# Moving the experts' first-layer products from the last group of an iteration to its first, in a two-layer attention and mixture-of-experts kernel

## What is computed

```python
xn = _layernorm(x)
s = attention(xn)                # 16 heads of 8 features, causal, softmax over 512 keys
gates = _top_k_softmax(cosine_scores(xn) + xn @ w_route.T, 2)        # 8 experts, top 2
h = jax.nn.gelu(jnp.einsum('bsd,edh->bseh', xn, w1) + b1, approximate=False)   # 8 experts x 64
expert_out = jnp.einsum('bseh,ehd->bsed', h, w2) + b2
g = _silu(jnp.einsum('bse,bsed->bsd', gates, expert_out))
x = x + s * g
xn = _layernorm(x)
s = xn + delta_rule_scan(layernorm_affine(xn))   # a 128x64 state, W -= lr (W k - v) k^T per token
g = _silu(xn @ sign(weight).T)
x = x + s * g
```

## Time and profile before

| | us |
|---|---|
| median of three runs | 613.15 |
| the three runs | 611.65, 613.15, 616.95 |
| time of the profiled execution | 617.68 |
| its span from first to last instruction | 616.0 |
| PE busy | 580.8 |
| DVE busy | 391.8 |
| ACT busy | 351.9 |

### The profile page before, as it was taken

One profiled execution on the slowest core, in us unless ns is written; L12 is line 12 of the kernel. 1 busy time (PEld: TensorE's weight loads), 2 busy tenths in 40 slices (PEclk: granted clock), 3 DMA queues, 4 the chain that ended last, 5 costly groups with the idle time before them and its releaser, 6 DMA issues.

```text
span 616.0 us, 17485 instructions
## 1 busy us (share of the span) xinstructions
PE 580.8 (94%) x7289; PEld 389.4 (63%) x7289; DVE 391.8 (64%) x975; ACT 351.9 (57%) x679; POOL 171.7 (28%) x335
## 2 busy tenths in 40 slices
PE   7799989899998999899999999899998999799897
PEld 3345564567575766677666766678576777565565
DVE  4488765767667676867666685767666675412453
ACT  4412556755675476756675466656675476676231
POOL 7157022412224221432223230432224200311121
PEclk9999999999998999999998999799998999999899
DMA  4766293847252115410362014410361000000001
GB/s 113 162 153 132 44 84 90 157 63 63 74 116 48 43 29 114 97 43 10 87 118 60 10 45 98 95 44 5 83 128 41 10 12 1 26 18 2 3 3 35
DMA packets 58163, 39.42 MB, mean 64 GB/s; under 512 B 17957, under 2 KB 57988, under 8 KB 58084
## 3 DMA queue, kind: packets, MB, share of 16 engines
q1 hardware_dynamic: 58051, 38.29, 30.9%
q10 hardware_dynamic: 32, 0.01, 0.0%
HBM read 24.46 MB, written 9.96 MB: 56 GB/s over the span
## 4 chain that ended last, share of the span: by engine, by line
PE 79%; DVE 11%; ACT 4%; issue 2%; DMA 1%; POOL 1%; SPq 0%; DVEq 0%; POOLq 0%
PE ps_v L950 13%; PE ps_s L930 11%; PE ps_e L911 6%; PE ps_a L865 5%; PE ps_a L851 4%; PE ps_c L1015 4%; DVE cand L1457 4%; PE ps_e L903 3%; PE ps_e L907 3%; PE ps_e L738 3%; PE ps_a L820 3%; PE ps_s L933 2%; PE ps_c L1099 1%; PE ps_c L997 1%; PE ps_c L984 1%
## 5 line engine op out<-in xcount | busy, mean ns | idle before, releaser
L1457 DVE TENSOR_REDUCE cand<-ps_s 128x4 f32<-128x512 f32 (+1 forms) x320 | 213.4, 685 | 74.4 <-PE ps_s L933 45.4
L1251 ACT ACTIVATE prob<-ps_e 128x512 f32<-128x512 f32 x320 | 188.4, 598 | 97.2 <-PE ps_e L911 55.7
L930 PE MATMUL ps_s<-kst,qst 72*128 72x128 bf16 (+2 forms) x1024 | 126.4, 236 | 15.8 <-DVE cand L1457 12.0
L930 PEld LDWEIGHTS ps_s<-kst,qst 72*128 72x128 bf16 (+1 forms) x1024 | 72.1, 98 | 77.5 <-DVE cand L1457 36.5
L911 PE MATMUL ps_e<-qst,kst 75*128 75x256 bf16 (+3 forms) x416 | 105.3, 284 | 0.0
L950 PE MATMUL ps_v<-prob,vaug 128*32 128x512 f32 (+3 forms) x1024 | 90.6, 455 | 0.0
L903 PE MATMUL ps_e<-identb,negmask 128*128 128x150 bf16 (+3 forms) x320 | 73.2, 229 | 3.7 <-ACT prob L1251 3.3
L907 PE MATMUL ps_e<-qst,kst 128*128 128x128 bf16 x384 | 75.8, 223 | 0.0
L911 PEld LDWEIGHTS ps_e<-qst,kst 75*128 75x128 bf16 x416 | 40.9, 98 | 3.5
L738 PE MATMUL ps_e<-identb 128*128 128x512 bf16 x115 | 40.5, 408 | 1.9 <-POOL identb L520 1.9
L907 PEld LDWEIGHTS ps_e<-qst,kst 128*128 128x128 bf16 x384 | 38.4, 100 | 4.6 <-issue 0.3
(11 more groups left out here) (340 smaller groups left out, 929.9 us busy)
## 6 DMA issues: line engine op xcount, KB each, us to landing
qst<-q_scratch SPq DMA_DIRECT2D x48, 192.0 KB
kst<-k_scratch SPq DMA_DIRECT2D x48, 192.0 KB
q_scratch<-qparts SPq DMA_DIRECT2D x24, 128.0 KB, 2.3
k_scratch<-kparts SPq DMA_DIRECT2D x24, 128.0 KB, 2.3
x_res<-in_L_attn_x_dram SPq DMA_DIRECT2D x8, 256.0 KB, 3.7
xn<-in_L_attn_x_dram SPq DMA_DIRECT2D x7, 256.0 KB, 3.5
out_dram<-second SPq DMA_DIRECT2D x7, 256.0 KB, 2.4
max_scratch<-mrow SPq DMA_DIRECT2D x16, 96.0 KB, 2.1
```

The lines of the kernel that those rows point to most:

```text
L930: last = mm(ps_s[:, bank, w * n:w * (n + 1)], q[0:rows, hd, tok(i)], k[0:rows, hd, keys[0]:keys[1]], start=(n == 0), stop=True, skip_group ...
L1251: af(prob[:, u, :], ps_e[:, u % 2, :], ACT.Exp).then_inc(S["e_emptied"], 1)
L1457: vec.tensor_reduce(cand[:, i, h0:h0 + FILLS * (len(hds) - 1) + 1:FILLS, S_SLOT[u]], ps_s[:, u % 2, :].rearrange("p (a c) -> p a c", a=len ...
```

## The change

`h0` to `h3` move from units (3,0), (3,2), (3,4) and (3,7) to units (0,1), (0,2), (0,3) and (0,4) of the same iteration. They then stand ahead of `gb0` to `gb3` and `out` of `cur`, which read the hidden values of the sequence before; for this `hid` becomes two tiles, chosen by the parity of the sequence. `gb0` to `gb3` take the units (0,8), (1,1), (1,4) and (1,6) instead of (0,1), (0,8), (1,1) and (1,4); `out` moves from (1,6) to (1,8), `xn2_norm` from (1,4) to (1,6), `c_xn2t` from (1,8) to (1,9), and `gt` from (1,9) to (2,3). `gelu` stays. The number of instructions of each kind does not change.

```diff
--- before.py
+++ after.py
@@ -58,14 +58,14 @@
 
 
 PLAN = {
-    (0, 0): ["c_u3"], (0, 1): ["gb0"], (0, 2): ["ln2_stats", "c_y3"], (0, 4): ["ln2_rstd", "hn_norm"],
-    (0, 6): ["pv0"], (0, 7): ["c_ht", "rn", "c_out"], (0, 8): ["gb1"], (0, 9): ["pv1", "c_kt", "c_qt"],
-    (1, 0): ["load_x", "m_rows1"], (1, 1): ["c_vk", "gb2"], (1, 2): ["c_gram", "pv2"], (1, 3): ["logits"],
-    (1, 4): ["yt", "gb3", "xn2_norm", "gates"], (1, 5): ["lev_a1", "gate_norm"], (1, 6): ["pv0", "out"], (1, 7): ["lev_d1"], (1, 8): ["c_xn2t"],
-    (1, 9): ["pv1", "lev_a2", "gt"], (2, 0): ["ln1_stats", "lev_d2", "ln1_rstd", "m_parts0"], (2, 1): ["c_ffn"], (2, 2): ["ln1_norm", "lev_a3", "pv2"], (2, 3): ["lev_d3"],
+    (0, 0): ["c_u3"], (0, 1): ["h0"], (0, 2): ["ln2_stats", "c_y3", "h1"], (0, 3): ["h2"], (0, 4): ["ln2_rstd", "hn_norm", "h3"],
+    (0, 6): ["pv0"], (0, 7): ["c_ht", "rn", "c_out"], (0, 8): ["gb0"], (0, 9): ["pv1", "c_kt", "c_qt"],
+    (1, 0): ["load_x", "m_rows1"], (1, 1): ["c_vk", "gb1"], (1, 2): ["c_gram", "pv2"], (1, 3): ["logits"],
+    (1, 4): ["yt", "gb2", "gates"], (1, 5): ["lev_a1", "gate_norm"], (1, 6): ["pv0", "gb3", "xn2_norm"], (1, 7): ["lev_d1"], (1, 8): ["out"],
+    (1, 9): ["pv1", "lev_a2", "c_xn2t"], (2, 0): ["ln1_stats", "lev_d2", "ln1_rstd", "m_parts0"], (2, 1): ["c_ffn"], (2, 2): ["ln1_norm", "lev_a3", "pv2"], (2, 3): ["gt", "lev_d3"],
     (2, 4): ["yt", "m_rows0"], (2, 5): ["lev_a4", "xnt"], (2, 6): ["pv0", "q", "lev_d4"], (2, 7): ["turned0"], (2, 8): ["lev_a5", "k"],
-    (2, 9): ["pv1", "lev_d5", "turned1"], (3, 0): ["stacks0", "h0", "low_blocks"], (3, 1): ["lev_a6"], (3, 2): ["h1", "lev_d6", "pv2"], (3, 3): ["c_u0"],
-    (3, 4): ["h2", "yt", "c_y0"], (3, 5): ["c_r1"], (3, 6): ["pv0", "c_u1"], (3, 7): ["c_y1", "h3"], (3, 8): ["c_r2"],
+    (2, 9): ["pv1", "lev_d5", "turned1"], (3, 0): ["stacks0", "low_blocks"], (3, 1): ["lev_a6"], (3, 2): ["lev_d6", "pv2"], (3, 3): ["c_u0"],
+    (3, 4): ["yt", "c_y0"], (3, 5): ["c_r1"], (3, 6): ["pv0", "c_u1"], (3, 7): ["c_y1"], (3, 8): ["c_r2"],
     (3, 9): ["c_u2", "pv1"], (4, 0): ["m_parts1", "gelu", "stacks1"], (4, 1): ["pv2", "c_y2"], (4, 2): ["v"], (4, 3): ["yt", "x1", "c_r3"],
 }
 
@@ -297,7 +297,7 @@
         grest = sb("grest", [P, NT, EXPERTS])
         gparts = sb("gparts", [P, NT, PARTS, QUAD], BF16)
         gT = sb("gT", [MAXROW, TOK], BF16)
-        hid = sb("hid", [P, NC, TOK])
+        hid = [sb(f"hid{p}", [P, NC, TOK]) for p in range(2)]
         tG = sb("tG", [P, TOK])
         cand = sb("cand", [P, NT, HEADS, 3])
         nm = sb("nm", [P, NT, HALF_HEADS])
@@ -862,7 +862,7 @@
                 pe.wait_ge(S["b2_ready"], PARTS)
                 for i in range(NT):
                     for c in range(NC):
-                        mm(ps_a[:, tok(i)], hid[:, c, tok(i)], w2s[:, c, :], start=(i == 0 and c == 0), stop=False,
+                        mm(ps_a[:, tok(i)], hid[b.parity][:, c, tok(i)], w2s[:, c, :], start=(i == 0 and c == 0), stop=False,
                            skip_group_check=True)
                     last = mm(ps_a[:, tok(i)], gT[:, tok(i)], b2s[:, :], start=False, stop=True, skip_group_check=True)
                 last.then_inc(S["a_filled"], 1)
@@ -1227,11 +1227,11 @@
             def h(b, c):
                 a_full(b, f"h{c}")
                 after(act, S["gelu_ready"], b.count(1, 0))
-                af(hid[:, c, :], ps_a[:, :], ACT.Identity, bias=vecT[:, c:c + 1]).then_inc(S["a_emptied"], 1)
+                af(hid[b.parity][:, c, :], ps_a[:, :], ACT.Identity, bias=vecT[:, c:c + 1]).then_inc(S["a_emptied"], 1)
 
             def gelu(b):
                 act.wait_ge(S["a_emptied"], A_NUMBER[b.c, "h3"] + 1)
-                af(hid[:, :, :], hid[:, :, :], ACT.Gelu).then_inc(S["gelu_ready"], 1)
+                af(hid[b.parity][:, :, :], hid[b.parity][:, :, :], ACT.Gelu).then_inc(S["gelu_ready"], 1)
 
             def out_piece(b):
                 a_full(b, "out")
@@ -1438,7 +1438,7 @@
             def gb(b, c):
                 a_full(b, f"gb{c}")
                 dve.wait_ge(S["gelu_ready"], b.count(1, 1))
-                vec.tensor_tensor(hid[:, c, :], hid[:, c, :], ps_a[:, :], ALU.mult).then_inc(S["a_emptied"], 1)
+                vec.tensor_tensor(hid[b.parity][:, c, :], hid[b.parity][:, c, :], ps_a[:, :], ALU.mult).then_inc(S["a_emptied"], 1)
 
             def out_piece(b):
                 dve.wait_ge(S["tg_ready"], b.count(1, 1))
```

## The result

The changed kernel takes **618.13 us** (median of 20 runs, 614.69 to 620.45), the kernel before **615.48 us** (20 runs beside them, 611.47 to 621.67). The ratio is 1.0044, with a 95% interval of 1.0023 to 1.0065: 0.4% slower. The profiled execution of after took 618.29 us with a span of 616.6, against 617.68 and 616.0. The forecast was 613.0.

What follows compares the result with a forecast made beforehand. The prediction took PE, busy for 94% of the span, to bound the kernel. From the profiled execution it summed 617.7 - 7.5 - 1.5 + 0.2 + 2.7 + 1.3 = 612.9, say 613 us, range 605 to 619.

Steps and rivals of the forecast that it cites:

- Cost +2.7: First iteration: `stacks0` issued 2.7 us later, so PE waits some 4.5 us instead of 1; +2.7 us (0 to 3.6).
- +0.2: Iteration from 114.9, the second: +0.2 us, since `older` isn't there and the old waits are shorter.
- +1.3: Behind the 4.5 us wait ahead of the second iteration: one low-clock stretch, +1.3 us (0 to 3).
- The normal iteration: Each normal iteration at full clock: 2.2 - 2.5 = -0.3 us; -1.5 us in all with the one from 458.2.
- group 0: Four products in, one gate product out, three waits at the one bank `ps_a`: grows by 2.2 us (1.6 to 3.0).
- group 3: Four products out, 3.6 us, less new waits of 0.85 and 0.25: shrinks by 2.5 us (1.9 to 3.6).
- The clock: Low stretches behind the 1.68 us waits go, as the new waits are 0.3 to 0.85 us: -7.5 us against the profiled execution.
- the one that the prediction names: Skill section "HAM oscillation — how this bites in real kernels": many short pauses can make the clock swing; left out of the sum.
- The base: Kernel before: median 613.15 us, taken as 4.5 us or three low stretches below the profiled time; 610.2 us without any.
- The new waits don't come: Rival, faster: an iteration gives 2.0 us instead of 0.3, so 600 us, half of it 605; chance 0.17.
- The clock falls in spite of it: Rival, slower: pauses in groups 0 and 3 bring one low stretch in every iteration, 9 us more, 622 us; chance 0.14.
- The wait of 1.01 isn't for `stacks0`: Rival on PE's wait before the second iteration: 2.7 and 1.3 fall away, 609 us; chance 0.14.

Runs made afterwards that it cites:

- the first experiments: The first four comparisons against the kernel before (615.76 us, 30 runs beside them), among them the old plan in the first iteration alone of the changed kernel, 610.39 us.
- the first experiment: Changed kernel with the old plan in its first iteration alone, measured against the kernel before: 610.39 us, ratio 0.9913.
- a seventh kernel: Changed kernel with the old first iteration, `low_blocks` at unit (2,7) and the products two units apart, against the kernel before: 608.3 us, ratio 0.9874.
- the two tiles alone: Changed kernel with the plan of the kernel before, so only the two `hid` tiles remain, against the kernel before: 615.56 us, ratio 0.999.

## Why the prediction was wrong

The forecast was no difference, 613 us; the chip says 0.4% slower, 618 us. The waits came where the prediction had put them; but it had the cost of the first iteration and of the low stretch behind it too small and the gain of a normal iteration too large, all on the same side, and its base was too low. On the profiled executions the sum was 612.9 and the time 618.3. The 5.4 us between them:

**The first iteration, 2.0 us: the step that failed.** "Cost +2.7" was +4.7 (60.16 against 55.43). I moved the issue of `stacks0` by what PE's order moves it, and took the time from issue to use as fixed at 11.5 us. That time has a part that isn't fixed. With `stacks1` issued 4.8 us behind it (107.43 and 112.22) it was 12.7 us, with `stacks1` held back 10.6, and the move of the issue was 3.2 us, not 2.7 (46.5 against 43.3 us from the first maximum). The wait was 5.47 us where I had 4.5, and the first unit behind it, at half the clock, came 0.3 us later to its maximum. The later issue, the 1.2 us more from issue to use and this make the 4.7. Nor were the 11.5 us typical of the old order. Of eight profiles with the old first iteration, five have PE going on 10.4 us after the issue without a wait; I had taken the number from one execution.

**The low stretch behind it, 0.6 us.** I had +0.2 and +1.3 for the second iteration, and it grew by 2.09. The +0.2 was right: with `stacks1` held back, and no low stretch in that profile, the iteration takes 67.67 us (116.77 to 184.44) against 67.47. So the stretch cost 1.9 us, not 1.3. It lasted 6.8 us and not 3.4; part of it lay inside the pause, where it costs nothing. With the first iteration undone, the time falls by 7.7 us by the medians and by 6.3 in the first two iterations of the profiles, where the prediction had 2.7 + 0.2 + 1.3 = 4.2. That is most of the distance between "a gain of 5 us" and "a loss of 3".

**The normal iteration, 2.2 us over five: the other term that was mis-sized.** It should have changed by -0.3 and changed by +0.17. The pieces, by group at full clock: group 0 +2.43 (I had +2.2), group 1 -0.24, group 2 +0.19, group 3 -2.22 (I had -2.5). In group 0 I made the loop through the one bank 1.80 us. It is 1.90, because ACT begins its copy 1.16 us after a product that came out of a wait has begun, not 1.05 (261.41 on PE, and here ACT), and such a product holds PE for 0.96 us:

```profile
262.57 0.69 ACT L1230 ACTIVATE hid<-ps_a,vecT 128x512 f32<-128x512 f32 x1 [0.73 <-PE ps_a L851]
```

In group 3 the waits at line 1041 and 1109 are there with 0.81 and 0.19 us (I had 0.85 and 0.25), but the products gave less than the 3.6 us that I had counted for them: from maximum to maximum, the units of `h1` and `h3` became 0.86 us shorter each, that of `h2` 0.48 and that of `h0` 0.01; with the two waits added back that is 3.2 us.

**The rest** is 1.5 us ahead of the first iteration, where the profiled execution of after has a low stretch at 26.6 and that of before has none (half the kernels' profiles have it, whatever their plan), and -0.9 at the end, where before has a low stretch at 573.8 and after none; the prediction had not counted that one. Neither is of the change.

**The clock, right.** The low stretches left the steady iterations, as forecast: before had four among five of them. The Trainium skill, page "TensorE: Matmul & The Clock Gate", lets one fear the opposite; it does so in its section "A second HAM failure mode: psum-queue depth-cycling", not in the one that the prediction names. The trace doesn't bear it out here: three pauses of 0.17 to 0.26 us around the products and one of 0.81 leave the clock at 1.00 in every steady iteration.

**The base.** The median of three runs, 613.15 us, was low. Over 20 and more runs the kernel before takes 615.5 to 616.4 us. The clocks on record say how many low stretches a run holds: the 30 runs beside the first experiments have a median clock of 0.986, which is 17 us at 1.2 GHz ((1 - 0.986) x 614 x 2) or five stretches of 3.4 us, not two. A straight line through their times and clocks gives 1.4 us for each stretch and, as an estimate, 608.7 us for a run without any, not 610.2. This turned no sign, but it made 613 look like "no change" when the sum against the profiled execution said 4.8 us faster. And the 1% that I took for the limit of the measurement was too wide: with 20 runs of each the interval is 0.2% either way.

**The rivals.** "The new waits don't come" fell with the rows at lines 851 and 1041. "The clock falls in spite of it" did not happen. "The wait of 1.01 isn't for `stacks0`" is refuted by the first experiment and the run with `stacks1` held back: the wait goes with the earlier issue, and shrinks when other loads are out of the way. No rival had the mechanism that decided it: the same wait for `stacks0`, dearer, with the low stretch behind it.

## What to carry to other kernels

Where a schedule has a steady part and a start, price the start by itself: a move that fills a wait in the steady part can push a load's issue in the one iteration in which nothing hides it, and a plan of its own for that iteration kept the gain of the steady part here. Time from the issue of a load to its use is no constant: see which other loads are issued within it. And in a steady loop like this one PE's longest pause is worth the most, since it costs itself and what the clock does behind it; to cut it to several under a microsecond paid here even though the waits' sum hardly changed.

## What the runs showed of the hardware

In the steady loop the low stretches come with PE's longest single pause. In the profiles of this study, iterations by their longest pause: up to 0.81 us, none of 30 with a low stretch (six kernels with the changed plan, five iterations each; a seventh kernel had none either, with one pause of 1.28 at a start); 1.08 us right behind one of 0.51, three of five; 1.08 to 1.23 us, one of seven; 1.67 to 1.68 us, nine of ten (before and the two tiles alone); 1.64 to 1.78 us, six of six. The second iteration is counted where it has such a pause. To lengthen one pause, at one place, took the count from none of six (0.66 to 0.81 us) over one (1.08 to 1.23) to six (1.64 to 1.78). PE's total idle time doesn't order them: with the products two units apart an iteration has 67.60 - 65.52 = 2.1 us and none of five a low stretch, while those of the kernel before at full clock have 1.9.

The start of the program repeats the experiment, unasked. There PE waits once for a load, for 1.50 to 2.46 us in the twelve profiles, here in after (timeline of PE):

```profile
25.88 0.40 PE L930 MATMUL ps_s<-kst,qst 72*128 72x128 bf16 x4 [2.10 <-DMA kst<-k_scratch]
```

The six profiles with 2.02 us and more have a low stretch right behind it, the six with 1.98 us and less have none. A small difference in this wait from one execution to the next can so decide some 1.4 us of the time (34.3 us in after from the first maximum at all to the first iteration, 32.7 in before, less the 0.3 us by which the wait is longer).

But the length that it takes isn't the same everywhere. Those six pauses of 1.50 to 1.98 us brought nothing, where 1.67 did in the loop; a pause of 1.63 us between 562 and 586 us, in all twelve profiles, has a low stretch behind it in one (before, at 573.8); and one of 0.98 us, between 518 and 540 us, has one in three of twelve. So it is likelihood, not law. The pauses of 5.05 to 5.47 us ahead of the second iteration brought a stretch of 6.8 us in all three profiles that have them, that of 3.39 us none in its one profile, but the clocks of the other 11 runs of that kernel say that it was the exception. What else decides it stays open; no run here varied it.

A low stretch of 3.4 us costs 1.3 to 1.5 us of time in the loop and one of 6.8 some 2.8 to 3.0, both less where PE would have waited anyway (some 0.9 us at 573.8).
